# Turning four of sixteen scan inputs with TensorE, and widening GpSimd's share of the products

## The chip, the cores and the metric

The kernel runs on one NeuronCore of a Trainium2 chip. The metric is the device time of one execution in microseconds. Engines are named PE (TensorE), DVE (VectorE), ACT (ScalarE), POOL (GpSimd) and SP (the engine that issues most DMAs).

## The reference

Two layers of a vision network of state-space scans work on x of 8 × 192 × 64 × 64. Each is `x + layer(group_norm(x))`. The first layer (layer 0 in the code, phase s0, 384 channels) projects and convolves the image, reads it in K = 4 directions of L = 4096 steps, and runs this scan for every channel d and each of N = 16 states n:

```python
delta = softplus(dt + bias)
h[n] = exp(delta * A[n]) * h[n] + (delta * u) * B[n]
y = sum over n of h[n] * C[n]
```

```python
ys = ys + Ds.reshape(K, Din)[None, :, :, None] * u
y = ys[:, 0] + ys[:, 2, :, ::-1]
yt = ys[:, 1] + ys[:, 3, :, ::-1]
```

yt is turned back to row order and added, and norm and projection follow. The second layer (layer 1 in the code, phase s1, 128 channels, 3 branches) runs the same sort of scan once per branch. B, C and the rank-12 part of dt come from a projection of u. Everything is fp32.

## The kernel before

The program is a chain of phases: features of the first layer, its scans, its output, then the same three for the second. `scan_phase` serves both layers. In the first, nd = 3 tiles of 128 channels lie side by side (J = 3), a step takes T = 512 time steps, and a **unit** g is one direction of one image in one chunk of 512 steps: 8 × 4 × 8 = 256 units, one after another. Units 0 to 7 of an image are direction 0, and so on; those of directions 2 and 3 "fold": they add the reversed result of directions 0 and 1, which is loaded again into `prev`. In the second layer J = 2 (two states at once), and there are 192 units of 8 states.

A unit of the first layer, for each of 16 states s:

- ACT computes the decays exp(delta × A) for 3 tiles, into a ring of DECAYS = 3 PSUM slots `dA` (L769). Decay (s, j) waits until the scan three tiles earlier is over.
- POOL forms `dbu` = du × B for 3 tiles at once (L845, 128 × 1536), AHEAD = 4 states in front of the scans. B comes as rows broadcast to 128 partitions by DMA into `b_sb`. Behind state s − 4's scans it multiplies that state's last tile by C (L855).
- DVE runs three scans (`tensor_tensor_scan`, L908, first operand decay, second dbu, start value `state`), and, behind the first scan of the next state, multiplies tiles 0 and 1 by C (L918; C in PSUM as `c_ps`). State 8 is an exception: POOL has no share, and DVE multiplies 3 tiles.
- PE spreads the C row over the partitions (L631), and sums h·C over the states into `y_ps` with identity matmuls: `state_sum` for DVE's products (L641), `pool_sum` for POOL's, three states later (L649).
- ACT saves the last column of h as the next unit's start value after every 2 states (L776).

Work for the next unit is placed by hand at states, in the dicts `on_pe`, `on_act`, `on_pool`: xproj (L587) at state 0 of PE and its copy at state 2 of ACT, dt (L605) at 3 to 5, softplus (L753, between two table loads L750 and L758) at 7, the three scalings of the identity by D (`scale_ident`, L721) at 8, corrections of the bf16 rows (`rest`, L595 and L596) at 8 and 10. POOL forms du = delta × u (L863) at 11. `direct` (L614) opens each unit's sum with D·u, for tiles 0 and 1 at state 1, for tile 2 at state 3, after ACT has copied the unit before out of PSUM (L732 at state 1, L738 at state 4), and L621 adds prev in folding units. ACT issues the store of `yo` at state 6.

All engines work in order. SP's queue does too: per unit it issues C part 1, prev (if the next unit folds), B part 2, the store of the next unit's rows, B part 3, C parts 2 and 3, B parts 0 and 1 and C part 0 of the next unit, then the loads of unit g + 2. A part is 4 rows × 512, broadcast to 1 MB. `h` holds 4 states, so a scan also waits for the products of four states before.

PE's order within a state:

```python
for s in range(NS):
    ...
    c_broadcast(g, s)
    if s == 1:
        direct(g, range(OWN), evacuated)
    if s:
        state_sum(g, s - 1)
    ...
    if nd > 1 and s == LAG:
        direct(g, (nd - 1,), evacuated_pool)
    if s >= LAG and s - LAG in SHARE:
        pool_sum(g, s - LAG)
```

## Time and profile before

| | |
|---|---|
| Time, median of 3 runs | 28,545.9 us (28,539.72 to 28,559.49) |
| Profiled execution, span | 28,546.6 us |
| DVE busy | 26,177.2 us (92%) |
| POOL busy | 24,984.9 us (88%) |
| PE busy | 23,745.5 us (83%), granted clock 0.970 |
| ACT busy | 15,919.5 us (56%) |
| All 15,296 recorded scans (L908) | 18,924.0 us |
| POOL's 5634 input products and du (L845) | 17,651.6 us |
| DMA | 4580.79 MB, mean 160 GB/s |

The span runs from the first to the last instruction, and stands within 1 us of the median time. A record's duration can overlap the next one's on the same engine by some hundredths to tenths of a microsecond, so two records' starts give the pace better than their durations. The scans of the first layer run from about 1070 to 20560 us of the span.

### The profile page before, as it was taken

What the parts mean: (1) busy time and instruction counts of PE and PEld (TensorE: products, weight loads), DVE (VectorE), ACT (ScalarE), POOL (GpSimd) and SP (SyncE); (2) the same over time, 40 slices, a digit from 0 to 9 for tenths busy, and PEclk for the clock granted to TensorE, in tenths of its full rate; (3) what the DMA queues carried; (4) which work ended last, traced back from release to release, by engine and by line L of the source; (5) the groups of instructions that cost most, each with busy time, mean ns of one, the idle gap of its engine ahead of it and who ended that gap; (6) DMA issues with size and microseconds to landing.
All of it is one profiled execution on the core that took longest, in us unless ns stands there. A gap on an engine that the chain in (4) does not pass through costs nothing. (4 is left out here: it accounts for less than half of the span.)

```text
span 28546.6 us, 217771 instructions
## 1 busy us (share of the span) xinstructions
PE 23745.5 (83%) x55698; PEld 9094.3 (32%) x55698; DVE 26177.2 (92%) x22479; ACT 15919.5 (56%) x25927; POOL 24984.9 (88%) x10936
## 2 busy tenths in 40 slices
PE   8778878887887887788788788878789988888888
PEld 3333333333333333333333333333334433333332
DVE  8899999999999999999999999999952179999996
ACT  2455555555555555555555555555522356666663
POOL 1699999999999999999999999999802179999995
PEclk9899999999999999999999999999999999999999
DMA  6533333333333333333333333333452357777778
GB/s 202 188 133 147 143 135 138 146 138 136 143 143 136 141 145 136 139 145 137 137 145 143 133 140 146 138 133 148 158 176 84 102 193 229 231 230 230 229 230 292
DMA packets 1193779, 4580.79 MB, mean 160 GB/s; under 512 B 254080, under 2 KB 291984, under 8 KB 827184
## 3 DMA queue, kind: packets, MB, share of 16 engines
q1 hardware_dynamic: 1093280, 4217.64, 41.8%
q10 hardware_dynamic: 99248, 349.22, 3.3%
q8 instruction: 450, 7.37, 0.1%
q14 instruction: 801, 6.56, 0.1%
HBM read 3907.76 MB, written 658.64 MB: 160 GB/s over the span
## 5 line engine op out<-in xcount | busy, mean ns | idle before, releaser
L908 DVE TENSOR_TENSOR_SCAN s_h<-s_dA,s_state,s_dbu 128x512 f32<-128x512 f32 x15296 | 18924.0, 1314 | 257.2 <-ACT s_dA L769 254.2
L845 POOL TENSOR_TENSOR s_dbu<-s_du,s_b_sb 128x1536 f32<-128x1536 f32 (+1 forms) x5634 | 17651.6, 3139 | 4.8 <-DVE s_h L908 3.1
L769 ACT ACTIVATE s_dA<-s_delta,s_negA 128x512 f32<-128x512 f32 x15360 | 10502.0, 690 | 8824.5 <-DVE s_h L908 8791.8
L641 PE MATMUL s_y_ps<-s_hc,s_ident 128*128 128x512 f32 x21504 | 10652.8, 617 | 1.5 <-DVE s_hc L918 1.5
L918 DVE TENSOR_TENSOR s_hc<-s_h,s_c_ps 128x1024 f32<-128x1024 f32 (+2 forms) x5632 | 6809.5, 1209 | 17.8 <-PE s_c_ps L631 12.3
L855 POOL TENSOR_TENSOR s_hc_pool<-s_h,s_c_sb 128x512 f32<-128x512 f32 x4608 | 5835.6, 1266 | 206.2 <-DVE s_h L908 202.3
L631 PE MATMUL s_c_ps<-s_bc,s_sel 96*128 96x512 bf16 x6400 | 2373.9, 390 | 3886.2 <-DVE s_hc L918 3883.7
L641 PEld LDWEIGHTS s_y_ps<-s_hc,s_ident 128*128 128x128 f32 x21504 | 4255.1, 198 | 3245.8 <-issue 3030.4
L649 PE MATMUL s_y_ps<-s_hc_pool,s_ident 128*128 128x512 f32 x9216 | 4789.6, 602 | 0.0
L631 PEld LDWEIGHTS s_c_ps<-s_bc,s_sel 96*128 96x128 bf16 x6400 | 569.2, 96 | 7635.9 <-DVE s_hc L918 6533.2
L649 PEld LDWEIGHTS s_y_ps<-s_hc_pool,s_ident 128*128 128x128 f32 x9216 | 1811.4, 197 | 2347.3 <-issue 2319.8
L1528 POOL TENSOR_TENSOR f_row_sum<-f_pad 96x1056 f32<-96x1056 f32 x64 | 155.1, 2424 | 1997.4 <-DVE f_pad L1475 1400.3
L863 POOL TENSOR_TENSOR s_du<-s_delta,s_u 128x1536 f32<-128x1536 f32 (+1 forms) x450 | 1126.5, 2503 | 190.1 <-ACT s_delta L756 146.0
L614 PE MATMUL s_y_ps<-s_u,s_D_ident 128*128 128x512 f32 x1920 | 973.8, 610 | 354.9 <-ACT s_yo L738 293.7
L605 PE MATMUL s_prep_ps<-s_xd,s_wdt 12*128 12x512 f32 (+1 forms) x1928 | 1083.7, 642 | 4.6 <-ACT s_bc L708 2.5
L1491 DVE TENSOR_TENSOR f_cen<-f_ps,f_middle 64x512 f32<-64x512 f32 x64 | 43.7, 682 | 1128.5 <-issue 672.2
L587 PE MATMUL s_prep_ps<-s_u,s_wx 128*108 128x512 f32 (+1 forms) x1928 | 910.6, 598 | 108.8 <-DMA s_keep_in<-in_keep 92.3
L776 ACT ACTIVATE s_state<-s_h,s_keep 128x6 f32<-128x6 f32 (+1 forms) x2432 | 724.2, 298 | 448.4 <-DVE s_h L908 439.7
L595 PE MATMUL s_prep_ps<-s_xd,s_twice 32*64 32x512 f32 x1800 | 963.9, 615 | 5.9 <-ACT s_delta L753 3.7
L311 DVE SCALAR_TENSOR_TENSOR f_row<-f_pad,f_taps,f_row 128x4096 f32<-128x4096 f32 x128 | 651.3, 5088 | 4.6
L750 ACT ACT_TABLE_LOAD x450 | 577.4, 1283 | 8.1
L758 ACT ACT_TABLE_LOAD x450 | 577.4, 1283 | 8.1
(162 smaller groups left out, 13497.4 us busy)
## 6 DMA issues: line engine op xcount, KB each, us to landing
s_b_sb<-rows SPq DMA_DIRECT2D x1794, 1024.0 KB, 5.0
s_c_sb<-rows SPq DMA_DIRECT2D x1216, 1024.0 KB, 6.6
s_u<-U SPq DMA_DIRECT2D x257, 768.0 KB
Y<-s_yo ACTq DMA_DIRECT2D x256, 768.0 KB, 5.5
s_prev<-Y SPq DMA_DIRECT2D x128, 768.0 KB, 6.1
s_u<-U SPq DMA_DIRECT2D x193, 256.0 KB
U<-f_row SPq DMA_DIRECT2D x24, 2048.0 KB, 17.3
U<-f_col SPq DMA_DIRECT2D x24, 2048.0 KB, 7.1
```

Source lines behind the costliest of these rows:

```text
L595: pe.matmul(prep_ps[0:64, :], twice[:, :], xd[0:32, :], start=True, stop=False)
L605: pe.matmul(prep_ps[:, :], wdt[g % 2][XROWS:XROWS + rank, t, :], xd[XROWS:XROWS + rank, :], start=True, stop=True).then_inc(dt_done, 1)
L614: last = pe.matmul(y_ps[:, t, :], D_ident[q][:, t, :], u[q][:, t, :], start=True, stop=False)
L631: last = pe.matmul(c_ps[:, r, :], sel[:, s * ng + r, :], bc16[g % 2][:, :], start=True, stop=True)
L641: last = pe.matmul(y_ps[:, t, :], ident[:, :], hc[:, s % 2, j, :], start=False, stop=nd > 1 and s == NS - 1)
L649: pe.matmul(y_ps[:, nd - 1, :], ident[:, :], hc_pool[:, (m - 1) % 4, :], start=False, stop=s == SHARE[-1]).then_inc(summed_pool, 1)
L769: act.activation(dA[:, n % DECAYS, :], delta[g % 2][:, t, :], ACT.Exp, scale=negA[g % 2][:, a:a + 1]).then_inc(dA_ready, 1)
L845: pool.tensor_tensor(dbu[:, s % AHEAD, :, :], a, b, ALU.mult).then_inc(dbu_ready, 1)
L855: pool.tensor_tensor(hc_pool[:, m % 4, :], h[:, s % (2 * GROUP), J - 1, :], c_sb[:, part % 2, row % ROWS_IN, :], ALU.mult).then_inc(hcp_re ...
L863: pool.tensor_tensor(du[q][:, :, :], delta[q][:, :, :], u[q][:, :, :], ALU.mult).then_inc(du_ready, 1)
L908: dve.tensor_tensor_scan(h[:, s % (2 * GROUP), j, :], dA[:, (n * J + j) % DECAYS, :], dbu[:, s % AHEAD, j, :], initial, ALU.mult, ALU.add) ...
L918: dve.tensor_tensor(hc[:, s % 2, 0:own, :], h[:, s % (2 * GROUP), 0:own, :], c, ALU.mult).then_inc(hc_ready, 1)
```

## The change

In the first layer's scans:

- States 3, 7, 11 and 14 (TURNED) no longer have their input formed by POOL. Once a unit, PE transposes the B and C rows (`turn_rows`) and the three tiles of du (`turn_du`), so that time lies on the partitions, and ACT copies them to SBUF (`take_rows`, `take_du`). For each turned state ACT multiplies the four blocks of 128 time steps of du by that state's B, which is then one value per partition (`scale_du`, 128 × 384, four per state), and PE transposes the result, tile by tile, back into a slot of the PSUM ring `dA` (`turn_input`, four transpositions per tile). The decays of these states go to SBUF (`dA_sb`), and the scan reads decay from SBUF and input from PSUM. `SCALE_AT` says at which states ACT does the scalings, `on_pe` and `on_act` where the turning of rows and du stands (states 11 to 15).
- POOL multiplies the last two tiles by C, in place of one, for states 2, 3, 6, 7, 10, 11 (TWO); state 8 now has a share like the others. DVE's products shrink by as many tiles.
- D is summed over the four directions and applied once, in direction 0's units; other units open their sum with prev or with the first product. The identity is scaled by D once per phase.
- `yo` and `prev` have one buffer in place of two, `hc` holds two tiles.

In the second layer TURNED and TWO are empty, and what remains is the single scaling of the identity and the one `yo`.

The diff, cut to what the prediction speaks of:

```diff
     C_STATES = tuple(range(NS)) if nd > 1 else (0, 2, 4, 6)
-    SHARE = tuple(s for s in C_STATES if nd == 1 or s != 8)
+    SHARE = C_STATES
     NSH = len(SHARE)
+    TWO = (2, 3, 6, 7, 10, 11) if nd > 1 else ()
+    POOL_TILES = 2 if nd > 1 else 1
     LAG = 3 if nd > 1 else 2
+    TURNED = (3, 7, 11, 14) if nd > 1 else ()
+    NT = len(TURNED)
+    PLAIN = tuple(s for s in range(NS) if s not in TURNED)
+    NPL = len(PLAIN)
+    QB = T // 128
+    SCALE_AT = {3: (0, 0, 1, 1), 7: (3, 4, 5, 5), 11: (7, 8, 9, 9), 14: (10, 11, 12, 12)}
...
-    on_pe = (dict(xproj=0, dt=(3, 4, 5), mid=8, low=10) if nd > 1 else
+    on_pe = (dict(xproj=0, dt=(3, 4, 5), mid=8, low=10, rows=11, turn_du=(12, 13, 14)) if nd > 1 else
              dict(xproj=0, dt=(2,), mid=4, low=5))
-    on_act = (dict(evacuate=1, take=2, evacuate_pool=4, dt=(4, 5, 6), store=6, soft=7, scale_ident=8, mid=9, low=11)
+    on_act = (dict(evacuate=1, take=2, evacuate_pool=4, dt=(4, 5, 6), store=6, soft=7, mid=9, low=11, rows=12, turn_du=(13, 14, 15))
               if nd > 1 else
-              dict(evacuate=2, take=2, soft=4, store=4, scale_ident=5, mid=6, low=7))
+              dict(evacuate=2, take=2, soft=4, store=4, mid=6, low=7))
     on_pool = dict(du=11 if nd > 1 else 7)
...
+    def opens(g):
+        return nd == 1 or g // NCH % K == 0
+    def opened_before(g):
+        return sum(1 for x in range(g) if opens(x))
+    def pool_tiles(s):
+        return 2 if s in TWO else 1 if s in SHARE else 0
     def in_product(s):
-        return J - 1 if s in SHARE else J
+        return J - pool_tiles(s)
...
+    def inputs_before(n):
+        return n // NS * NPL + sum(1 for x in PLAIN if x < n % NS)
+    def state_of_input(i):
+        return i // NPL * NS + PLAIN[i % NPL]
...
-        yo = [sb(f"yo{q}", [128, nd, T]) for q in range(2)]
-        D_ident = [sb(f"D_ident{q}", [128, nd, 128]) for q in range(2)]
-        prev = [sb(f"prev{q}", [128, nd, T]) for q in range(2 if BACK else 0)]
+        yo = sb("yo", [128, nd, T])
+        D_in, D_ident = sb("D_in", [128, K, nd]), sb("D_ident", [128, nd, 128])
+        if BACK:
+            prev = sb("prev", [128, nd, T])
+        if NT:
+            duT, rowsT = sb("duT", [128, QB, nd * 128]), [sb(f"rowsT{q}", [128, QB, 32]) for q in range(2)]
+            scaled_du, dA_sb = sb("scaled_du", [128, 2, QB, nd * 128]), sb("dA_sb", [128, J, T])
...
                 f, other = fold_of(g), partner(g)
-                wait(eng, prev_summed, f - 1)
-                eng.wait_ge(stored[other % 2], 16 * (other // 2 + 1))
-                eng.dma_start(prev[f % 2][:, :, :], Y[other]).then_inc(prev_in[f % 2], 16)
+                wait(eng, prev_summed, f)
+                eng.wait_ge(stored, 16 * (other + 1))
+                eng.dma_start(prev[:, :, :], Y[other]).then_inc(prev_in, 16)
...
-                wait(eng, dbu_ready, g * NS + (part + 1 - B_RING) * STEPS_IN)
+                wait(eng, dbu_ready, inputs_before(g * NS + (part + 1 - B_RING) * STEPS_IN))
...
+            def turn_rows(g):
+                pe.wait_ge(xd_ready, g + 1)
+                pe.wait_ge(bc_ready, g * 3 + 3)
+                for b in range(QB):
+                    last = pe.transpose(prep_ps[:, b * 32:(b + 1) * 32], xd[0:32, b * 128:(b + 1) * 128], ident[0:32, 0:32])
+                last.then_inc(rows_turned, 1)
+            def turn_du(g, t):
+                pe.wait_ge(du_ready, g + 1)
+                if t == 0:
+                    pe.wait_ge(rows_taken, g + 1)
+                else:
+                    pe.wait_ge(du_taken, g * nd + t)
+                for b in range(QB):
+                    last = pe.transpose(prep_ps[:, b * 128:(b + 1) * 128], du[g % 2][:, t, b * 128:(b + 1) * 128], ident[:, :])
+                last.then_inc(du_turned, 1)
+            def turn_input(g, s, j):
+                m, n = turn_of(g, s), (g * NS + s) * J + j
+                pe.wait_ge(du_scaled, (m + 1) * QB)
+                wait(pe, scanned, n - DECAYS + 1)
+                for b in range(QB):
+                    last = pe.transpose(dA[:, n % DECAYS, b * 128:(b + 1) * 128],
+                                        scaled_du[:, m % 2, b, j * 128:(j + 1) * 128], ident[:, :])
+                last.then_inc(input_turned, 1)
             def direct(g, tiles, read):
-                q = g % 2
-                pe.wait_ge(D_ready, g + 1)
                 wait(pe, read, g)
-                for t in tiles:
-                    last = pe.matmul(y_ps[:, t, :], D_ident[q][:, t, :], u[q][:, t, :], start=True, stop=False)
-                if tiles[-1] == nd - 1:
-                    last.then_inc(direct_done, 1)
+                if opens(g):
+                    for t in tiles:
+                        last = pe.matmul(y_ps[:, t, :], D_ident[:, t, :], u[g % 2][:, t, :], start=True, stop=False)
+                    if tiles[-1] == nd - 1:
+                        last.then_inc(direct_done, 1)
                 if folds(g):
-                    f = fold_of(g)
-                    pe.wait_ge(prev_in[f % 2], 16 * (f // 2 + 1))
+                    pe.wait_ge(prev_in, 16 * (fold_of(g) + 1))
                     for t in tiles:
-                        last = pe.matmul(y_ps[:, t, :], ident[:, :], prev[f % 2][:, t, ::-1], start=False, stop=False)
+                        last = pe.matmul(y_ps[:, t, :], ident[:, :], prev[:, t, ::-1], start=True, stop=False)
...
-                pe.matmul(y_ps[:, nd - 1, :], ident[:, :], hc_pool[:, (m - 1) % 4, :],
-                          start=False, stop=s == SHARE[-1]).then_inc(summed_pool, 1)
+                tiles = pool_tiles(s)
+                for i in range(tiles):
+                    last = pe.matmul(y_ps[:, nd - tiles + i, :], ident[:, :], hc_pool[:, (m - 1) % 4, i, :],
+                                     start=begins(g, s), stop=s == SHARE[-1])
+                last.then_inc(summed_pool, 1)
...
+                    if NT and s == on_pe["rows"]:
+                        turn_rows(g + 1)
+                    if NT and s in on_pe["turn_du"]:
+                        turn_du(g + 1, on_pe["turn_du"].index(s))
+                    if s + 1 in TURNED:
+                        turn_input(g, s + 1, 0)
                     c_broadcast(g, s)
                     if s == 1:
                         direct(g, range(OWN), evacuated)
                     if s:
                        state_sum(g, s - 1)
                     elif g:
                         state_sum(g - 1, NS - 1)
+                    if s + 1 in TURNED:
+                        turn_input(g, s + 1, 1)
                     if nd > 1 and s == LAG:
                         direct(g, (nd - 1,), evacuated_pool)
                     if s >= LAG and s - LAG in SHARE:
                         pool_sum(g, s - LAG)
                     elif s < LAG and g and NS + s - LAG in SHARE:
                         pool_sum(g - 1, NS + s - LAG)
+                    if s + 1 in TURNED:
+                        turn_input(g, s + 1, 2)
...
+            def take_rows(g):
+                act.wait_ge(rows_turned, g + 1)
+                act.activation(rowsT[g % 2][:, :, :], prep_ps[:, 0:QB * 32].rearrange("p (b n) -> p b n", n=32),
+                               ACT.Copy).then_inc(rows_taken, 1)
+            def take_du(g, t):
+                act.wait_ge(du_turned, g * nd + t + 1)
+                wait(act, du_scaled, g * NT * QB)
+                act.activation(duT[:, :, t * 128:(t + 1) * 128], prep_ps[:, :].rearrange("p (b d) -> p b d", d=128),
+                               ACT.Copy).then_inc(du_taken, 1)
+            def scale_du(g, s, b):
+                m = turn_of(g, s)
+                act.wait_ge(rows_taken, g + 1)
+                act.wait_ge(du_taken, (g + 1) * nd)
+                wait(act, input_turned, (m - 1) * J)
+                act.activation(scaled_du[:, m % 2, b, :], duT[:, b, :], ACT.Copy,
+                               scale=rowsT[g % 2][:, b, s:s + 1]).then_inc(du_scaled, 1)
...
-                wait(act, stored[q], 16 * (g // 2))
-                place = yo[q][:, 0:OWN, ::-1] if folds(g) else yo[q][:, 0:OWN, :]
+                wait(act, stored, 16 * g)
+                place = yo[:, 0:OWN, ::-1] if folds(g) else yo[:, 0:OWN, :]
...
-                wait(act, scanned, n - DECAYS + 1)
+                if s in TURNED:
+                    m = turn_of(g, s)
+                    if m:
+                        act.wait_ge(scanned, turned_state(m - 1) * J + j + 1)
+                    place = dA_sb[:, j, :]
+                else:
+                    wait(act, scanned, n - DECAYS + 1)
+                    place = dA[:, n % DECAYS, :]
                 a = t * N_STATE + s * ng + r
-                act.activation(dA[:, n % DECAYS, :], delta[g % 2][:, t, :], ACT.Exp,
+                act.activation(place, delta[g % 2][:, t, :], ACT.Exp,
...
-                wait(pool, scanned, (n - AHEAD + 1) * J)
+                i = inputs_before(n)
+                if i >= AHEAD:
+                    pool.wait_ge(scanned, (state_of_input(i - AHEAD) + 1) * J)
                 a, b = du[g % 2][:, :, :], b_sb[:, s % (B_RING * STEPS_IN), :, :]
                 a, b = (a, b.broadcast_to([128, nd, T])) if ng == 1 else (a.broadcast_to([128, ng, T]), b)
-                pool.tensor_tensor(dbu[:, s % AHEAD, :, :], a, b, ALU.mult).then_inc(dbu_ready, 1)
+                pool.tensor_tensor(dbu[:, i % AHEAD, :, :], a, b, ALU.mult).then_inc(dbu_ready, 1)
...
-                pool.tensor_tensor(hc_pool[:, m % 4, :], h[:, s % (2 * GROUP), J - 1, :],
-                                   c_sb[:, part % 2, row % ROWS_IN, :], ALU.mult).then_inc(hcp_ready, 1)
+                tiles = pool_tiles(s)
+                c = c_sb[:, part % 2, row % ROWS_IN:row % ROWS_IN + 1, :].broadcast_to([128, tiles, T])
+                pool.tensor_tensor(hc_pool[:, m % 4, 0:tiles, :], h[:, s % (2 * GROUP), J - tiles:J, :], c,
+                                   ALU.mult).then_inc(hcp_ready, 1)
...
-                    input_of(g + s // NS, s % NS)
+                    if s % NS in PLAIN:
+                        input_of(g + s // NS, s % NS)
...
+                if s in TURNED:
+                    dve.wait_ge(input_turned, turn_of(g, s) * J + j + 1)
+                    decay, given = dA_sb[:, j, :], dA[:, (n * J + j) % DECAYS, :]
+                else:
+                    i = inputs_before(n)
+                    decay, given = dA[:, (n * J + j) % DECAYS, :], dbu[:, i % AHEAD, j, :]
+                    if j == 0:
+                        dve.wait_ge(dbu_ready, i + 1)
...
-                dve.tensor_tensor_scan(h[:, s % (2 * GROUP), j, :], dA[:, (n * J + j) % DECAYS, :],
-                                       dbu[:, s % AHEAD, j, :], initial, ALU.mult, ALU.add).then_inc(scanned, 1)
+                dve.tensor_tensor_scan(h[:, s % (2 * GROUP), j, :], decay, given, initial,
+                                       ALU.mult, ALU.add).then_inc(scanned, 1)
```

## Rows read from the trace of the kernel before

**Rows 1.** Stretch table, 6000 to 12000 us: busy us (x count) by engine, then clock.

```profile
6000.00:12000.00 6000.00, 4836.43 (x10912) 1849.91 (x10911) 5921.34 (x5045) 3540.24 (x5829) 6000.00 (x2523) 0.97 0.37 139
```

**Rows 2.** Groups of instructions by shape, 6000 to 18000 us: busy us, mean ns, idle.

```profile
L908 DVE TENSOR_TENSOR_SCAN s_h<-s_dA,s_state,s_dbu 128x512 f32<-128x512 f32 x7566 | 9183.4, 1273 | 158.3 <-ACT s_dA L769 155.3 <-POOL s_dbu L845 3.0
...
L845 POOL TENSOR_TENSOR s_dbu<-s_du,s_b_sb 128x1536 f32<-128x1536 f32 x2523 | 8665.9, 3435 | 0.0
...
L641 PEld LDWEIGHTS s_y_ps<-s_hc,s_ident 128*128 128x128 f32 x10401 | 2077.2, 200 | 1646.9 <-issue 1580.3
...
L721 ACT ACTIVATE s_D_ident<-s_ident,s_small 128x128 f32<-128x128 f32 x471 | 153.2, 388 | 0.0
...
L738 ACT ACTIVATE s_yo<-s_y_ps 128x512 f32<-128x512 f32 x157 | 90.9, 579 | 0.0
```

**Rows 3.** Timeline of DVE around state 8 of a unit: start us, us.

```profile
10027.97 2.46 DVE L908 TENSOR_TENSOR_SCAN s_h<-s_dA,s_state,s_dbu 128x512 f32<-128x512 f32 x2
10031.44 1.28 DVE L908 TENSOR_TENSOR_SCAN s_h<-s_dA,s_state,s_dbu 128x512 f32<-128x512 f32 x1 [1.01 <-ACT s_dA L769]
10032.64 1.20 DVE L918 TENSOR_TENSOR s_hc<-s_h,s_c_ps 128x1024 f32<-128x1024 f32 x1
10033.75 3.63 DVE L908 TENSOR_TENSOR_SCAN s_h<-s_dA,s_state,s_dbu 128x512 f32<-128x512 f32 x3
10037.30 1.73 DVE L918 TENSOR_TENSOR s_hc<-s_h,s_c_ps 128x1536 f32<-128x1536 f32 x1
10038.94 3.63 DVE L908 TENSOR_TENSOR_SCAN s_h<-s_dA,s_state,s_dbu 128x512 f32<-128x512 f32 x3
```

**Rows 4.** Timeline of POOL, one state of the first layer.

```profile
9003.82 1.26 POOL L855 TENSOR_TENSOR s_hc_pool<-s_h,s_c_sb 128x512 f32<-128x512 f32 x1
9005.05 3.42 POOL L845 TENSOR_TENSOR s_dbu<-s_du,s_b_sb 128x1536 f32<-128x1536 f32 x1
9008.44 1.26 POOL L855 TENSOR_TENSOR s_hc_pool<-s_h,s_c_sb 128x512 f32<-128x512 f32 x1
```

**Rows 5.** Groups by shape in the second layer, 22000 to 28546 us.

```profile
L845 POOL TENSOR_TENSOR s_dbu<-s_du,s_b_sb 128x1024 f32<-128x1024 f32 x1537 | 3583.2, 2351 | 4.6 <-DVE s_h L908 3.1 <-DMA s_b_sb<-rows 1.5
...
L918 DVE TENSOR_TENSOR s_hc<-s_h,s_c_ps 128x1024 f32<-128x1024 f32 x768 | 1079.6, 1406 | 2.1 <-PE s_c_ps L631 1.4 <-DVE s_h L908 0.7
...
L918 DVE TENSOR_TENSOR s_hc<-s_h,s_c_ps 128x512 f32<-128x512 f32 x768 | 669.4, 872 | 10.7 <-PE s_c_ps L631 10.7
```

**Rows 6.** Timeline of ACT from decay (6,2) to decay (8,0), the same unit as rows 3.

```profile
10021.16 0.69 ACT L769 ACTIVATE s_dA<-s_delta,s_negA 128x512 f32<-128x512 f32 x1 [0.48 <-DVE s_h L908]
...
10021.79 0.67 ACT L744 ACTIVATE s_work<-s_prep_ps,s_small 128x512 f32<-128x512 f32 x1
10022.36 0.29 ACT L776 ACTIVATE s_state<-s_h,s_keep 128x6 f32<-128x6 f32 x1
...
10026.53 1.28 ACT L750 ACT_TABLE_LOAD   x1
...
10029.32 1.28 ACT L758 ACT_TABLE_LOAD   x1
10030.62 1.92 ACT L769 ACTIVATE s_dA<-s_delta,s_negA 128x512 f32<-128x512 f32 x3
```

**Rows 7.** Timeline of PE, one state: an x4 row is four matmul records.

```profile
9001.42 1.88 PE L641 MATMUL s_y_ps<-s_hc,s_ident 128*128 128x512 f32 x4
9003.14 1.02 PE L649 MATMUL s_y_ps<-s_hc_pool,s_ident 128*128 128x512 f32 x2
...
9006.58 0.38 PE L631 MATMUL s_c_ps<-s_bc,s_sel 96*128 96x512 bf16 x1
9006.80 1.88 PE L641 MATMUL s_y_ps<-s_hc,s_ident 128*128 128x512 f32 x4
```

**Rows 8.** DMA issues, 6000 to 18000 us: count, size, median us to landing.

```profile
s_b_sb<-rows SPq DMA_DIRECT2D x631, 1024.0 KB, 4.7
...
s_prev<-Y SPq DMA_DIRECT2D x80, 768.0 KB, 6.1
```

More of the change, by code:

```diff
@@ L462, in scan_phase @@
         loaded = [sem(f"loaded{q}") for q in range(2)]
-        stored = [sem(f"stored{q}") for q in range(2)]
+        stored = sem("stored")
         xproj_done, rest_done, bc_ready, minus_set = sem("xproj_done"), sem("rest_done"), sem("bc_ready"), sem("minus_set")
@@ L574, in _ @@
                         broadcast_b(g + 1, 3)
-            for q in range(2):
-                eng.wait_ge(stored[q], 16 * (units // 2))
+            eng.wait_ge(stored, 16 * units)
             eng.wait_ge(rows_stored, 16 * (units + 1))
@@ L623, in direct, with begins @@
                         last.then_inc(prev_summed, 1)
+            def begins(g, s):
+                return s == 0 and not opens(g) and not folds(g)
             def c_broadcast(g, s):
@@ L641, in state_sum @@
                     last = pe.matmul(y_ps[:, t, :], ident[:, :], hc[:, s % 2, j, :],
[L642 removed]
+                                     start=begins(g, s), stop=nd > 1 and s == NS - 1)
                 last.then_inc(summed, 1)
@@ L683, in _ @@
                 rest(0, part)
+            if NT:
+                turn_rows(0)
+                for t in range(nd):
+                    turn_du(0, t)
             for g in range(units):
@@ L811, in unit @@
                         take_rest(g + 1, 1)
+                    if NT and s == on_act["rows"]:
+                        take_rows(g + 1)
+                    for x in TURNED:
+                        for b in range(QB):
+                            if SCALE_AT[x][b] == s:
+                                scale_du(g, x, b)
+                    if NT and s in on_act["turn_du"]:
+                        take_du(g + 1, on_act["turn_du"].index(s))
                     if s == on_act["store"] and g:
@@ L820, in _ @@
             softplus(0)
-            scale_ident(0)
             for part in range(2):
                 take_rest(0, part)
+            if NT:
+                take_rows(0)
+                for t in range(nd):
+                    take_du(0, t)
             for g in range(units):
@@ L884, in _ @@
         def _(dve):
-            dve.wait_ge(const_in, 32)
+            dve.wait_ge(const_in, 48)
+            for k in range(1, K):
+                dve.tensor_tensor(D_in[:, 0, :], D_in[:, 0, :], D_in[:, k, :], ALU.add).then_inc(D_summed, 1)
+                dve.wait_ge(D_summed, k)
+            dve.sem_inc(D_summed, 1)
             dve.tensor_copy(sel[:, :, :].rearrange("p a b -> p (a b)"), self32).then_inc(sel_ready, 1)
```

74 lines of the change are left out of this document (41 added, 33 removed).

## The prediction

> **What bounds the kernel now.** I read the stretch table first, then the groups of instructions, then the timelines of single engines. From 6000 to 12000 us VectorE (DVE) is busy for 5921 us and GpSimd (POOL) for all 6000, while ScalarE (ACT) has 3540 and TensorE (PE) 4836, at a granted clock of 0.97 of 2.4 GHz [rows 1]. 7566 scans stand in 12,000 us; a unit has 48, so a unit takes 12,000 × 48 / 7566 = 76.13 us, and layer 0's 256 units take 19.5 of the 28.5 ms [rows 2].
>
> VectorE: three scans start within 3.55 us (1.183 each), a product of two tiles takes 1.11 and one of three tiles 1.64 [rows 3]. 48 × 1.183 + 15 × 1.11 + 1.64 = 75.1 us, and before the scan of state 8 it waits 1.01 us for a decay [rows 3]: 76.1. GpSimd: product 1.23 us, input product 3.39 us from start to start [rows 4]; du is taken as an input product. 16 × 3.39 + 15 × 1.23 + 3.39 = 76.1. Both are full, but the scans waited 155 us for ScalarE and only 3 us for GpSimd [rows 2]: VectorE's own sequence, with its wait, sets the period, and GpSimd keeps pace with nothing to spare. A change has to relieve both.
>
> **The change, part by part.** I write S_n for the start of state n's first scan on VectorE. A state takes 3.55 + 1.11 = 4.66 us; where the product inside it (that of the state before) has one tile it is shorter.
>
> VectorE. Six states give a second tile's product to GpSimd, and state 8 gives its first. Removing a tile saves 1.64 − 1.11 = 0.53 us [rows 3]; the narrow product itself is not in layer 0, but in layer 1 it differs from the wide one by 1406 − 872 = 534 ns [rows 5]. 7 × 0.53 = 3.7 us. The narrow product is then 0.58, and the state around it takes 4.13. Scans of the four turned states read the decay from SBUF and the input from PSUM, the reverse of now. No row shows that; the bounds are zero and one narrow product's reading (0.53 us, 12 times, 6 us); I take zero, since such a scan still reads one tile from each memory, as today's does. VectorE without waits: 75.1 − 3.7 = 71.4.
>
> GpSimd. Four inputs go, −4 × 3.39 = −13.6. State 8's product comes, +1.23; six products become two tiles wide, each by half of 3.39 − 1.23 = 2.16, so +1.08 and +6.5 (layer 1's input product of two tiles, 2351 ns, agrees with 1.23 + 1.08 [rows 5]). 76.1 − 13.6 + 7.7 = 70.2: below VectorE.
>
> ScalarE. A scaling of 128 columns takes 388 ns as a record [rows 2], the decay of 512 columns 690 [rows 6]; for 384 columns that gives 0.59, some 0.5 from start to start. 16 of these (9.4), three copies of du (0.58 each, as L738's copy of 512 columns out of PSUM [rows 2]), one of the rows (0.25), less three scalings of the identity (1.2): +10.2 on 3540 / 6000 × 76.13 = 44.9 [rows 1], so 55 of 71: hidden by sum. By order: today the softplus with its two table loads (4.09 us) sits behind decay (7,2), which can only start when its PSUM slot is free; that is the wait of 1.01 us. State 7 is now turned and its decays go to SBUF, so they needn't wait for a scan. The first row of rows 3 holds scans (7,1) and (7,2), so S_6 was 10027.97 − 2.29 − 4.66 = 10021.02, and decay (6,2) starts at S_6 + 0.14 [rows 6]; then follow dt copy and state save (0.8 in all), three decays (1.85), tables and softplus (4.09), the first scaling for state 11 (0.5), and decay (8,0), ready at about S_6 + 8.85. State 8 is due at S_6 + 4.66 + 4.13 = S_6 + 8.79. So 0.1 us of the 1.01 stays. What is late next is the scaling work; I went through ACT's order state by state, and every other scaling stands at least 2 us ahead of the transposition that takes it.
>
> TensorE. Two matmul records make one fp32 product of 512 columns; four start within 1.72 us, so 0.43 each, and a bf16 one takes 0.22 [rows 7]. A unit now has 48 products of h·C (41.3 us), 3 of u with x_proj, 3 of dt, 3 direct, on average 1.5 of the earlier result (9.0), 16 C rows in bf16 (3.5) and two corrections (2.2): 56.0. Three of four direct groups go: 54.1. Added: 60 transpositions of 128 × 128 and 4 short ones, at x each. The trace of before has none. Lower bound: a quarter of 0.22, 0.055. Upper: two passes, each a weight load of 0.20 [rows 2] and 128 columns (0.107) in turn, 0.61. I take one pass of 128 columns at fp32's pace, 0.107, nearest to the row of the same type: weight loads lie beside running matmuls in rows 7 (four start within 1.72 us though each has its load), and I take it that the second pass of an fp32 product serves the multiplication, which a transposition has not. Sum 54.1 + 64 × 0.107 = 61 of 71.
>
> The Trainium skill (TensorE: Matmul & The Clock Gate, Part 4: PE-mode transpose) speaks against this: some 390 ns for a bf16 transpose alone and 275 in a kernel, and the full clock isn't engaged by transposes. By 0.275, an estimate, TensorE's sum would be 71.7, above VectorE's. Its section Terms calls transpose mode four times faster for fp32, which would give 0.053 by rows 7. No row here decides between them.
>
> TensorE's order matters more than its sum, as three transposed tiles per turned state are interleaved with other products, and VectorE waits for each. Tightest is state 11. From the end of product 8 at S_9 + 2.3: C row 0.22, state_sum(8) 1.72, pool_sum(6) 1.72 (two tiles now), rest 1.08, four transpositions, C row 0.22, state_sum(9) 1.72, four transpositions, pool_sum(7) 1.72, four transpositions: 8.4 + 12x. Tile 2's scan is due at S_11 + 2.95 = S_9 + 12.3, so 10.0 are there: x up to 0.13 costs nothing. At 0.107 the margin is 0.3 us; I allow 0.1 for hand-overs. The same count gives 5.1 + 16x against 8.1 for state 14 (up to 0.19, with du's transposition ahead), 8x against 1.6 for state 7 (0.20) and 7.3 + 12x against 10.0 for state 3 (0.22).
>
> SP queue. With one prev buffer, load_prev(g+1) waits until prev of unit g is summed, about S_4 + 2.3 (ScalarE's evacuation after decay (4,2), then two passes). Queued behind it are B's part 2, the row store, B's part 3 and C's part 2. A B part lands 4.7 us after issue and prev 6.1 [rows 8]; in a row I put B's part at S_4 + 10. GpSimd would like it at S_5 + 1.3, so it comes to stand 4 to 5 us late; by its own times (70.2 a unit) input 12 is where that lateness is nearest to the scans, and it reaches them if the part lands after about S_4 + 11. I count 0. It can concern 120 of 256 units (those that fold and are followed by one that folds). The single yo buffer: the store of unit g−1 is issued at state 6 and lands before the next evacuation, most of a unit later: nothing. Layer 1 loses one scaling of 0.39 us per unit on ScalarE, which waits for scans there: nothing. The start gains some 5 us of turning, once.
>
> **Sum.** 71.4 + 0.1 + 0.1 = 71.6 us a unit, 4.53 less; × 256 = 1160; + 5. The profiled execution's 28,546.6 becomes 27,392; I say 27,400. Its span is within 1 us of the median of 28,545.9.
>
> **Rivals.**
> - *The wait on ScalarE stays* because the added scalings cost more than 0.5 or start late: +0.9 us a unit, 27,630. For: the chain at state 8 has no reserve. Against: the decays of state 7 are freed by a whole state. Chance 0.14.
> - *Transpositions take two passes*, x = 0.21: state 11 is 1.0 late, 14 0.4, 7 0.1: +1.4 after the 0.1 allowed, 27,760. For: every fp32 product in rows 7 does so. Chance 0.14.
> - *The held SP queue starves GpSimd*: a landing 3 us after the limit costs 120 × 3 = 360 us, 27,760. For: three 1 MB transfers and prev come in one burst. Chance 0.08.
> - *Other side: TensorE's turning sets the period.* If weight load and columns follow one another, x = 0.20 + 0.107 = 0.30; the late tiles cost 2.0 (state 11), 1.8 (14), 0.8 (7), 0.7 (3, in three of four units): 5.3, so 76.8 us a unit and 28,720. It decides from x = 0.28, where the waits eat all 4.5 us; in two passes of 0.21 TensorE's sum alone would be 81, 29,900. For: each transposition has another weight, of 0.20 us. Against: loads lie beside matmuls today. Chance 0.06. The skill's 0.275 as a price is this rival's edge, the waits 4.2 us, 28,490; for it I keep 0.03.
> - *The inputs aren't relieved* (scans slower from swapped memories): 0.02.
>
> The forecast has 0.53. The range: below, 27,300, if the scans or products come out 0.3 us a unit cheaper; above, 27,800, which takes in the first three rivals and leaves out some 0.13. Under 0.2% (57 us) a measurement can't tell from no change. Faster 0.92, same 0.02, slower 0.06.
>
> **What would show it.** In the new profile: scans of layer 0 at 1.18 apart also for the four turned states; narrow products of 0.58 apart; GpSimd with idle time in front of products, released by scans; transpose records and their spacing (0.107 or 0.21); VectorE's waits by releaser: on dA by ScalarE near 0.1 us a unit, on the transposed tiles near 0.1 at state 11, on dbu none. Waits of 1 us and more on transposed tiles show TensorE's rivals; waits on dbu in units 17 to 31 of each image, with b_sb landing late, the SP queue. I am wrong if the unit is longer than 72.5 us.

## The result and the profile after

The changed kernel takes 27,906.65 us (median of 4 runs, 27,883.81 to 27,921.66) against 28,545.42: a ratio of 0.9775, with a 95% interval of 0.9763 to 0.9787. It is faster by 639 us, where 1146 were forecast, and lies above the range. Times here are medians of a kernel's undisturbed executions; one of the four of e2_prev_late took 61,744 us at a granted clock of 0.41 and is left out.

Engines' totals on the page of the profiled execution (span 27,919.9 us):

```profile
PE 24874.1 (89%) x70946; PEld 10612.0 (38%) x70946; DVE 25291.2 (91%) x22482; ACT 17866.2 (64%) x30091; POOL 23560.1 (84%) x10168
```

The stretch table, as in [rows 1]: VectorE busy 5835 of 6000, GpSimd no longer full, TensorE from 4836 to 5367.

```profile
6000.00:12000.00 6000.00, 5367.45 (x16151) 2401.87 (x16150) 5835.04 (x5211) 4297.78 (x7405) 5744.51 (x2364) 0.98 0.38 144
```

Groups by shape, 6000 to 18000 us, as in [rows 2]. 5863 scans of plain states, 36 a unit, make a unit of 12,000 × 36 / 5863 = 73.7 us, against 76.13 before and 71.6 forecast.

```profile
L1049 DVE TENSOR_TENSOR_SCAN s_h<-s_dA,s_state,s_dbu 128x512 f32<-128x512 f32 x5863 | 7151.4, 1265 | 38.2 <-ACT s_dA L884 32.3 <-POOL s_dbu L971 2.4
...
L1049 DVE TENSOR_TENSOR_SCAN s_h<-s_dA_sb,s_state,s_dA 128x512 f32<-128x512 f32 x1955 | 2438.0, 1266 | 191.0 <-PE s_dA L672 188.9 <-ACT s_dA L884 1.8
...
L830 ACT ACTIVATE s_scaled_du<-s_duT,s_rowsT 128x384 f32<-128x384 f32 x2606 | 1496.6, 605 | 6.1
...
L672 PE MATMUL s_dA<-s_ident,s_scaled_du 128*128 128x128 f32 x7819 | 1183.2, 274 | 26.6 <-DVE s_h L1049 26.6
...
L672 PEld LDWEIGHTS s_dA<-s_ident,s_scaled_du 128*128 128x128 f32 x7817 | 954.7, 141 | 934.5 <-issue 905.6 <-ACT s_scaled_du L830 26.9
```

The scans of turned states take as long as the others (1266 and 1265 ns), a scaling 605 ns. Each transposition is one matmul record of 274 ns and one weight load of 141. VectorE's timeline in a unit of direction 1, as in [rows 3], at state 11:

```profile
9169.53 1.25 DVE L1049 TENSOR_TENSOR_SCAN s_h<-s_dA_sb,s_state,s_dA 128x512 f32<-128x512 f32 x1
9170.70 0.66 DVE L1059 TENSOR_TENSOR s_hc<-s_h,s_c_ps 128x512 f32<-128x512 f32 x1
9171.28 1.27 DVE L1049 TENSOR_TENSOR_SCAN s_h<-s_dA_sb,s_state,s_dA 128x512 f32<-128x512 f32 x1
9172.95 1.28 DVE L1049 TENSOR_TENSOR_SCAN s_h<-s_dA_sb,s_state,s_dA 128x512 f32<-128x512 f32 x1 [0.40 <-PE s_dA L672]
```

The narrow product runs from 9170.70 to the next scan's start at 9171.28, 0.58 us, and the third turned scan waits 0.40 us for its transposed input. That is the one recorded wait in this unit, which takes 71.9 us. Its price is a little more than the wait: 1.67 us lie between the starts of the second and the third scan (9171.28 to 9172.95) where 1.18 is the pace, so 0.49. Waits in total, 6000 to 18000 us (us, times, longest):

```profile
POOL s_dbu L971 <- DMA s_b_sb<-rows: 264.5, 75, 4.7
...
DVE s_h L1049 <- PE s_dA L672: 188.9, 357, 3.0
...
PE s_prep_ps L626 <- DMA s_keep_in<-in_keep: 108.9, 67, 3.2
...
DVE s_hc L1059 <- issue: 90.7, 64, 3.9
...
DVE s_h L1049 <- ACT s_dA L884: 34.0, 45, 0.9
```

VectorE waits 188.9 us for transposed inputs and 90.7 in front of products, where nothing else is named than the missing C row. With the smaller ones it is 329 us in 163 units, 2.0 us a unit.

**Units by direction.** ACT starts the softplus once a unit; the distance from one start to the next, averaged by the direction to which the unit belongs, is this (us; 64 units each, 63 for direction 0):

| kernel | dir. 0 | dir. 1 | dir. 2 | dir. 3 | time, us |
|---|---|---|---|---|---|
| before | 76.19 | 76.13 | 76.14 | 76.13 | 28,545 |
| changed | 73.48 | 72.86 | 74.22 | 74.10 | 27,907 |
| e3_turn_first | 71.64 | 72.23 | 73.93 | 74.17 | 27,753 |
| e4_fill | 71.89 | 71.90 | 73.93 | 74.20 | 27,738 |
| e1_evac3 | 72.23 | 72.19 | 72.45 | 72.56 | 27,592 |
| e2_prev_late | 73.72 | 72.93 | 73.48 | 73.71 | 27,889 |
| e8_fill_prev | 71.89 | 71.90 | 71.90 | 71.90 | 27,480 |
| e7_all | 71.65 | 71.64 | 71.79 | 71.64 | 27,424 |
| e9_all_fill | 71.38 | 71.39 | 71.39 | 71.39 | 27,348 |
| e5_no_two | 74.43 | 74.47 | 74.46 | 74.46 | 28,127 |
| e10_before_fill | 76.18 | 76.13 | 76.41 | 76.41 | 28,582 |

Directions 2 and 3 fold and load prev, direction 0 applies D, direction 1 does neither. In the changed kernel some units of directions 0 and 1 take 71.9 us, others 75.0. Here is PE in one of the latter, of direction 0:

```profile
10611.71 1.74 PE L681 MATMUL s_y_ps<-s_u,s_D_ident 128*128 128x512 f32 x2 [1.35 <-ACT s_yo L846]
10613.24 1.92 PE L721 MATMUL s_y_ps<-s_hc_pool,s_ident 128*128 128x512 f32 x2
10615.09 1.31 PE L644 MATMUL s_prep_ps<-s_xd,s_wdt 12*128 12x512 f32 x2
10616.33 0.39 PE L701 MATMUL s_c_ps<-s_bc,s_sel 96*128 96x512 bf16 x1
...
10636.00 0.61 PE L701 MATMUL s_c_ps<-s_bc,s_sel 96*128 96x512 bf16 x1 [2.48 <-DVE s_hc L1059]
10636.40 3.37 PE L711 MATMUL s_y_ps<-s_hc,s_ident 128*128 128x512 f32 x4
```

An idle stretch of 1.35 us, waiting for the evacuation of tile 2, ends at 10611.71. The two records that follow start 1.53 us apart from the next row in place of 0.86, and two more take until 10615.09. At 10636.40 four records have 3.37 us where four had 1.88. The stretch table of the same unit says why; the number after the five engines is the granted clock:

```profile
9130.00:9202.00 72.00, 62.84 (x195) 28.07 (x194) 71.57 (x65) 52.99 (x92) 70.69 (x30) 1.00 0.37 141
...
10611.70:10615.30 3.60, 3.59 (x5) 1.19 (x6) 3.60 (x4) 3.11 (x6) 2.74 (x2) 0.55 0.62 214
...
10636.00:10639.40 3.40, 3.40 (x5) 1.67 (x6) 3.40 (x3) 2.23 (x4) 3.40 (x3) 0.50 1.01 417
```

0.50 is TensorE at 1.2 GHz in place of 2.4, for some 3.5 us, twice in this unit. Both times it had stood idle just before (1.35 and 2.48 us). In the unit of 9130 us it stands idle 1.64 us at the first of these places and 2.55 us at the second (9162.64, shown further down), and there the clock stays at 1.00 (first row of the table): not every such pause is followed by a fall. PE in that unit, with four transpositions between a `state_sum` and a `pool_sum`, and the pause:

```profile
9134.00 0.60 PE L672 MATMUL s_dA<-s_ident,s_scaled_du 128*128 128x128 f32 x4
9134.44 1.02 PE L721 MATMUL s_y_ps<-s_hc_pool,s_ident 128*128 128x512 f32 x2
...
9139.78 1.12 PE L721 MATMUL s_y_ps<-s_hc_pool,s_ident 128*128 128x512 f32 x2 [1.64 <-ACT s_yo L846]
```

What VectorE waits for in the unit of 10600 us:

```profile
10616.81 1.22 DVE L1059 TENSOR_TENSOR s_hc<-s_h,s_c_ps 128x1024 f32<-128x1024 f32 x1 [1.10 <-issue]
...
10628.25 1.28 DVE L1049 TENSOR_TENSOR_SCAN s_h<-s_dA_sb,s_state,s_dA 128x512 f32<-128x512 f32 x1 [0.25 <-PE s_dA L672]
...
10643.45 1.28 DVE L1049 TENSOR_TENSOR_SCAN s_h<-s_dA_sb,s_state,s_dA 128x512 f32<-128x512 f32 x1 [0.48 <-PE s_dA L672]
...
10645.82 1.28 DVE L1049 TENSOR_TENSOR_SCAN s_h<-s_dA_sb,s_state,s_dA 128x512 f32<-128x512 f32 x1 [0.52 <-PE s_dA L672]
10647.98 1.28 DVE L1049 TENSOR_TENSOR_SCAN s_h<-s_dA_sb,s_state,s_dA 128x512 f32<-128x512 f32 x1 [0.88 <-PE s_dA L672]
```

The first loss of some 1.7 us of matmul time shows up as 1.10 us before a product and 0.25 at state 7; the second makes all three tiles of state 11 late, 0.48 + 0.52 + 0.88 us. Together 3.2, where the unit at 9130 us loses 0.40.

In stretches of 1 us between 9000 and 11500 us, the kernel before has 46 falls below 0.95 of the clock in 33 units, and its units of directions 1 to 3 all take 76.12 to 76.15 us. The changed one has 27 in 34 units. The falls aren't new; there was nothing that waited for them. Over all units of the first layer but the first and the last the changed kernel has 67 falls in direction 0, 29 in direction 1, 52 in 2 and 69 in 3.

### The profile page after: what moved, and what is told of

The parts are those of the page before. It is cut to its first block and busy times, and to the rows that moved or that the text cites. A ratio compares the mean times of both kernels' runs of the same rounds, so it can differ in the third digit from the quotient of the medians.

```text
span 27919.9 us, 261599 instructions
## 1 busy us (share of the span) xinstructions
PE 24874.1 (89%) x70946; PEld 10612.0 (38%) x70946; DVE 25291.2 (91%) x22482; ACT 17866.2 (64%) x30091; POOL 23560.1 (84%) x10168
## 5 line engine op out<-in xcount | busy, mean ns | idle before, releaser
L1049 DVE TENSOR_TENSOR_SCAN s_h<-s_dA,s_state,s_dbu 128x512 f32<-128x512 f32 x12236 | 14960.7, 1269 | 59.2 <-ACT s_dA L884 50.7
L971 POOL TENSOR_TENSOR s_dbu<-s_du,s_b_sb 128x1536 f32<-128x1536 f32 (+1 forms) x4610 | 14188.6, 3084 | 430.9 <-DMA s_b_sb<-rows 428.7
L884 ACT ACTIVATE s_dA<-s_delta,s_negA 128x512 f32<-128x512 f32 x12288 | 8289.9, 685 | 5515.3 <-DVE s_h L1049 5501.6
L711 PE MATMUL s_y_ps<-s_hc,s_ident 128*128 128x512 f32 x17920 | 8785.2, 602 | 1.5 <-DVE s_hc L1059 1.5
L983 POOL TENSOR_TENSOR s_hc_pool<-s_h,s_c_sb 128x512 f32<-128x512 f32 (+1 forms) x4864 | 7843.8, 1617 | 575.4 <-DVE s_h L1049 514.6
L1059 DVE TENSOR_TENSOR s_hc<-s_h,s_c_ps 128x1024 f32<-128x1024 f32 (+1 forms) x5632 | 5526.0, 981 | 169.5 <-issue 140.9
L1049 DVE TENSOR_TENSOR_SCAN s_h<-s_dA_sb,s_state,s_dA 128x512 f32<-128x512 f32 x3060 | 3816.0, 1266 | 295.1 <-PE s_dA L672 290.8
L830 ACT ACTIVATE s_scaled_du<-s_duT,s_rowsT 128x384 f32<-128x384 f32 x4096 | 2352.4, 605 | 9.6
L884 ACT ACTIVATE s_dA_sb<-s_delta,s_negA 128x512 f32<-128x512 f32 x3072 | 1982.1, 710 | 0.0
L672 PE MATMUL s_dA<-s_ident,s_scaled_du 128*128 128x128 f32 x12288 | 1859.3, 274 | 42.6 <-DVE s_h L1049 42.6
```

Source lines behind the costliest of these rows:

```text
L672: last = pe.transpose(dA[:, n % DECAYS, b * 128:(b + 1) * 128], scaled_du[:, m % 2, b, j * 128:(j + 1) * 128], ident[:, :])
L711: last = pe.matmul(y_ps[:, t, :], ident[:, :], hc[:, s % 2, j, :], start=begins(g, s), stop=nd > 1 and s == NS - 1)
L830: act.activation(scaled_du[:, m % 2, b, :], duT[:, b, :], ACT.Copy, scale=rowsT[g % 2][:, b, s:s + 1]).then_inc(du_scaled, 1)
L884: act.activation(place, delta[g % 2][:, t, :], ACT.Exp, scale=negA[g % 2][:, a:a + 1]).then_inc(dA_ready, 1)
L971: pool.tensor_tensor(dbu[:, i % AHEAD, :, :], a, b, ALU.mult).then_inc(dbu_ready, 1)
L983: pool.tensor_tensor(hc_pool[:, m % 4, 0:tiles, :], h[:, s % (2 * GROUP), J - tiles:J, :], c, ALU.mult).then_inc(hcp_ready, 1)
```

## The experiments

Four explanations of the 2.1 us a unit that separate 73.7 from 71.6 stood against one another: falls of TensorE's clock, which push its transposed tiles and C rows past a thin margin (theory 1); the SP queue held by prev, with loads that come late (2); the order of TensorE's work alone, late at any clock (3); and TensorE's load as such, which more work would make worse (4).

**e3_turn_first.**

```diff
+                    if s + 1 in TURNED:
+                        turn_input(g, s + 1, 2)
                     if s >= LAG and s - LAG in SHARE:
                         pool_sum(g, s - LAG)
...
-                    if s + 1 in TURNED:
-                        turn_input(g, s + 1, 2)
```

> Only PE's order differs from the changed kernel: a turned state's third tile is transposed ahead of the pool_sum of that state, which takes 1.72 us out of the chain that the scan waits for. Theory 1 (half-clock stretches of TensorE make it late, and the chains have too little margin to absorb 1.7 us): the margin grows from 0.3 to about 2 us, so most late third tiles go, in units with a half-clock stretch too: about 27,600 us, with waits of scans for transposed tiles under 0.6 us a unit. Theory 2 (the held SP queue brings loads late): no help in the units that fold, 27,800. Theory 3 (only the thin margin at state 11, 0.4 us in every unit): 27,907 - 256 x 0.4 = 27,805.

27,753 us (ratio 0.9721, 0.9706 to 0.9735), a gain of 153, between theories 1 and 3. By direction it is clearer: directions 0 and 1 gain 1.8 and 0.6 us a unit, more than the 0.5 of state 11, direction 2 gains 0.3 and direction 3 nothing. Waits for transposed inputs fall from 188.9 to 56.7 us. Not all of it is margin: direction 0 has 14 falls of the clock here where the changed kernel has 67. Direction 1 has more of them, 62 against 29, and is faster all the same, so the wider margin does absorb falls. The folding units have another trouble.

**e4_fill**, with `zeros` a bf16 tile of zeros, 0.22 us a matmul.

```diff
+            def keep_busy(count):
+                for _ in range(count if nd > 1 else 0):
+                    pe.matmul(y_ps[:, 0, :], zeros[:, 0:128], zeros[:, :], start=False, stop=False)
...
+                    if s == 9:
+                        keep_busy(9)
                     c_broadcast(g, s)
...
+                    if s == LAG:
+                        keep_busy(6)
```

> Adds 15 bf16 matmuls of zeros by zeros per unit of the first layer (0.22 us each, 3.3 us a unit) where PE stands idle: 6 ahead of the direct group at state 3, 9 ahead of the C row of state 9. They add zero to the sums. Theory 1 (clock): the half-clock stretches behind these two idle places become rare, and although TensorE has 3.3 us more work a unit the time falls, to about 27,650. Theory 4 (TensorE is simply short of time at full clock): more work makes it slower, 28,000 or more. Theory 2 (SP queue): unchanged within 60 us of 27,907.

27,738 us (0.9714, 0.9700 to 0.9729). TensorE does 3.3 us more a unit and the kernel is 169 us faster. All units of directions 0 and 1 but the first take 71.89 to 71.92 us, so theory 4, TensorE's load as such, falls, and the clock holds for them (no fall in either direction, 34 and 41 in directions 2 and 3): the waits left there are the 0.40 of state 11. Directions 2 and 3 stay at 74. What waits there is now mostly the product:

```profile
DVE s_hc L1070 <- issue: 103.2, 48, 4.7
DVE s_h L1060 <- PE s_dA L673: 66.0, 165, 0.4
```

**e1_evac3.**

```diff
-    on_act = (dict(evacuate=1, take=2, evacuate_pool=4, ...
+    on_act = (dict(evacuate=1, take=2, evacuate_pool=3, ...
```

> Only ACT's order differs: the evacuation of tile 2 stands at state 3 in place of 4, so PE no longer waits 1.0 to 1.6 us for it in state 3, and prev is summed some 3 us earlier. Theory 1 (clock): the idle place ahead of the direct group goes, with it the half-clock stretches that begin there, and PE reaches state 5 earlier; the product of state 4 no longer waits for its C row: 27,650 to 27,700. Theory 2: gains only in units that fold, where load_prev is released earlier, 27,750. Theory 3: 27,907, as state 11 is untouched.

27,592 us (0.9663, 0.9646 to 0.9679), a gain of 315, more than theory 1 gave. All directions gain, the folding ones too, as PE isn't stopped at state 3 and prev is free earlier (GpSimd's waits on b_sb fall from 264.5 to 136.9 us). It changes both causes at once and doesn't tell them apart; as a repair it is the best single line.

**e2_prev_late.**

```diff
-                    if folds(g + 1):
-                        load_prev(g + 1)
                     broadcast_b(g, 2)
                     store_rows(g + 1)
                     broadcast_b(g, 3)
+                    if folds(g + 1):
+                        load_prev(g + 1)
```

> Only SP's order differs: load_prev(g+1) is issued behind B part 3 in place of ahead of B part 2, so its wait for the single prev buffer holds nothing up. Theory 2 (the held queue is the cause): waits of POOL for b_sb and of xproj for the loads vanish and the time falls to 27,450. Theory 1 (clock): those waits vanish, but the late tiles stay, above all in direction 0, which loads no prev: 27,850, a gain of at most 0.5 us in half of the units.

27,889 us (0.9766, 0.9750 to 0.9782), not to be told from the changed kernel by the intervals. The folding units gain 0.7 and 0.4 us, the others lose 0.2 and 0.1. TensorE's waits for the loads are all but gone (the row of its weight loads, the only one left, has 7.2 us):

```profile
DVE s_h L1049 <- PE s_dA L672: 214.5, 412, 3.0
...
DVE s_hc L1059 <- issue: 78.0, 71, 1.1
...
PEld s_prep_ps L626 <- DMA s_keep_in<-in_keep: 7.2, 20, 1.0
```

Taken alone this says that the SP queue costs next to nothing. It does cost something, as seen next.

**e8_fill_prev**, the two together.

> The matmuls of zeros of e4_fill together with the SP order of e2_prev_late. With the first alone directions 0 and 1 came to 71.9 us a unit in every unit and directions 2 and 3 stayed at 74; with the second alone nothing moved by more than 0.7. Theory 5 (two causes, each of which hides the other in directions 2 and 3: half-clock stretches, and loads that come late behind the held SP queue): together all four directions come to 71.9, 27,907 - 256 x (73.55 - 71.9) = 27,480. If a third cause keeps directions 2 and 3 slow, they stay above 73 and the time above 27,650.

27,480 us (0.9626, 0.9609 to 0.9642), as expected, and all four directions at 71.9. The granted clock is 1.00, and the waits:

```profile
6000.00:18000.00 12000.00, 11242.17 (x35286) 5090.87 (x35618) 11928.56 (x10682) 8814.26 (x15190) 11783.90 (x4841) 1.00 0.39 148
```

```profile
DVE s_h L1060 <- PE s_dA L673: 66.8, 167, 0.4
...
PE s_prep_ps L627 <- DMA s_keep_in<-in_keep: 1.4, 2, 0.7
```

66.8 us in 167 units is the 0.40 of state 11, and no other wait of VectorE is recorded. Against e4_fill the same edit of the queue that gained 18 us alone, within the noise, now gains 258; against e2_prev_late the filling gains 409, where alone it gained 169. Each cause hid the other in the folding units.

How the queue does harm, in a folding unit of the changed kernel. The first row holds two B parts; SP stays at the second until 9621.93. Behind it come a C part and the loads (u, and as the last keep):

```profile
9601.32 20.61 SPq L566 DMA_DIRECT2D s_b_sb<-rows  x2
...
9622.50 0.38 SPq L537 DMA_DIRECT2D s_u<-U  x1
...
9624.47 0.44 SPq L541 DMA_DIRECT2D s_keep_in<-in_keep  x1
```

PE's xproj needs them and waits 2.82 us. It then takes 4.36 us for six records, 0.73 each where 0.43 is the pace, so this pause too is followed by a lower clock; only behind it comes the C row of state 0:

```profile
9632.38 4.52 PE L626 MATMUL s_prep_ps<-s_u,s_wx 128*108 128x512 f32 x6 [2.82 <-DMA s_keep_in<-in_keep]
9636.74 0.38 PE L701 MATMUL s_c_ps<-s_bc,s_sel 96*128 96x512 bf16 x1
```

VectorE at the same place:

```profile
9628.82 1.26 DVE L1049 TENSOR_TENSOR_SCAN s_h<-s_dA,s_state,s_dbu 128x512 f32<-128x512 f32 x1
...
9637.22 1.22 DVE L1059 TENSOR_TENSOR s_hc<-s_h,s_c_ps 128x1024 f32<-128x1024 f32 x1 [2.48 <-issue]
```

State 0 begins at 9628.82 and the product of state 0 has waited 2.48 us for its C row. The loads were issued 6.3 us before the state began; in the unit of direction 1 at 9130 us they are issued at 9181.75, 10.5 us before the next unit's state 0. The B part ahead of them waits for the unit's last input product, and that GpSimd forms late because an earlier B part reached it late, behind the held load of prev (264.5 us of waits on b_sb in the changed kernel). Putting prev behind the B parts removes this chain.

**e7_all**: evac3, prev late and turn first, no added work.

> No added work: the evacuation of tile 2 at state 3, load_prev behind B part 3, and the third tile's transposition ahead of pool_sum, all three. Theory 5 says that the margin now absorbs a half-clock stretch and that the loads are in time: 71.4 to 71.6 us a unit in all directions, 27,380 (the forecast's 27,400). If half-clock stretches still cost, 27,500.

27,424 us (0.9607, 0.9593 to 0.9621). The least unit is 71.38, the means by direction are 71.64 to 71.79: between the two cases.

**e9_all_fill**, e7_all with nine matmuls of zeros at state 9.

> e7_all with 9 matmuls of zeros ahead of the C row of state 9 (2.0 us a unit). e7_all's units took 71.64 on the mean and 71.38 at the least; what is left above 71.38 are units with a half-clock stretch. Theory 1: all units come to 71.4 and the time to 27,424 - 256 x 0.25 = 27,360. If not, 27,424 as before, or more by the added work.

27,348 us (0.9580, 0.9566 to 0.9594), every unit but the first 71.38 to 71.40 us, and no wait of VectorE is recorded between 6000 and 18000 us (busy 11,995 of 12,000). Direction 1 still has 22 falls of the clock, and its units take no longer: with this order they cost nothing. It beats both kernels, the changed one by 559 us, and is VectorE's own sum with 0.1 us at state 8 (see below).

**e10_before_fill.**

> The kernel before, with the 15 matmuls of zeros of e4_fill per unit of the first layer. Theory 1 says that half-clock stretches cost nothing there, since no scan waits for TensorE and its C rows are early: the granted clock rises from 0.97 towards 1 and the time stays within 30 us of 28,546. If half-clock stretches cost the kernel before as well, the time falls by some of the 1.7 us x 1.4 stretches a unit, by up to 600 us.

28,582 us (1.0014, 1.0004 to 1.0023), 36 us slower, 6 more than expected; and the clock rose only from 0.970 to 0.975, so the run can't tell what a full clock would bring there. Units of directions 2 and 3 grow by 0.27 us; in half of the units ScalarE now waits 0.2 us for dt, which it didn't before, so the added work is the likely reason. That falls of the clock were free in the kernel before rests on its own units of 76.12 to 76.15 us instead.

**e5_no_two and e6_no_turned**, one half of the change each:

```diff
-    TWO = (2, 3, 6, 7, 10, 11) if nd > 1 else ()
+    TWO = ()
```

> The change without its wider share: TWO is empty, the turned states and everything else stay. By the sums, VectorE's unit is 75.1 - 0.5 (state 8's tile) = 74.6 us without waits and GpSimd's 63.7; PE's margin per state grows by half a microsecond where the states are longer. 28,546 - 256 x (76.13 - 74.7) = 28,180. If the turned states' scans were themselves dearer, it would be above 28,300.

28,127 us (0.9853, 0.9834 to 0.9873). All units but two take 74.4 to 74.5 us, in all directions, although GpSimd waits for b_sb here as well (260 us between 6000 and 18000). With the narrow share VectorE's unit is longer, and what is late in the changed kernel comes in time here. The clock has a part in that: it is 1.00 without any filling, with falls in direction 1 alone (20), and the run doesn't tell longer states from the fuller clock.

```profile
6000.00:18000.00 12000.00, 10465.50 (x31988) 4667.40 (x31987) 11999.36 (x10314) 8532.07 (x14662) 10355.88 (x4674) 1.00 0.38 143
```

```diff
-    TURNED = (3, 7, 11, 14) if nd > 1 else ()
+    TURNED = ()
```

> The change without turned states: TURNED is empty, GpSimd forms all 16 inputs and has the wider share as well. By the sums its unit is 76.1 + 7.7 = 83.8 us, above VectorE's 71.4, and it sets the period: 28,546 + 256 x 7.7 = 30,500. If GpSimd were not bound so tightly, below 29,500.

30,504 us, a single execution, against 30,500. GpSimd is busy for all 12,000 us between 6000 and 18000, and VectorE now waits for inputs and for products:

```profile
DVE s_hc L1059 <- issue: 755.0, 197, 5.9
DVE s_h L1049 <- POOL s_dbu L971: 699.9, 591, 3.8
```

The two halves aren't alike. The turned states, with D's and state 8's edits, gain 1.5% without the wider share; the wider share without the turned states costs 7%. Together they gain 2.2% as changed, and 4.2% where nothing is late (e9_all_fill).

## Why the prediction was wrong

- **VectorE's sum, right.** 71.4 us a unit without waits was forecast; 71.38 to 71.39 is the least unit of e3, e7 and e9 (its first unit aside), with some 0.1 of waiting at state 8 in it, so 71.3. The scans with swapped memories cost nothing more (1266 against 1265 ns), the narrow product 0.58.
- **GpSimd's sum, right.** e6_no_turned tests it with the wider share alone: 83.8 a unit forecast, 83.8 in the mean, counted as in the table, and 30,504 us where 30,500 was expected. In the changed kernel it is busy 70.5 us a unit where 70.2 was forecast.
- **ScalarE, right.** A scaling takes 605 ns (0.59 forecast), and ScalarE is busy 53 us in the unit of 9130 us (55 forecast). Of the 1.01 us at state 8, 0.1 was to stay, and 0.1 stays, too little for a wait to be recorded. The first scan of state 8 starts at 9156.07, 2.49 us behind the two before it where such a pair takes 2.37, just after its decay, the first of the three at 9155.26 (0.69 us), is ready; e8_fill_prev and e9_all_fill show the same 0.1:

```profile
9153.58 2.45 DVE L1049 TENSOR_TENSOR_SCAN s_h<-s_dA_sb,s_state,s_dA 128x512 f32<-128x512 f32 x2
9156.07 1.28 DVE L1049 TENSOR_TENSOR_SCAN s_h<-s_dA,s_state,s_dbu 128x512 f32<-128x512 f32 x1
...
9155.26 1.89 ACT L884 ACTIVATE s_dA<-s_delta,s_negA 128x512 f32<-128x512 f32 x3
```

- **The price of a transposition, right.** Four start within 0.44 us (9134.00 to 9134.44 above), so x = 0.11 against 0.107. The rival with two passes falls, and so does serial loading. The Trainium skill's 275 ns, for a bf16 transpose in a kernel (TensorE: Matmul & The Clock Gate, Part 4: PE-mode transpose), isn't the pace here but nearly the length of one fp32 record, 274 ns. That page also says that transposes don't engage the full clock. It can't be seen here: e8_fill_prev has 64 of them a unit at a granted clock of 1.00, but they stand between ordinary matmuls, and no run shows them alone.
- **TensorE's chain at state 11, the step that failed.** "8.4 + 12x against 10.0, the margin is 0.3 us" was worked out at full clock, with 0.1 us allowed for hand-overs. Two things were missing. First, the terms. PE in the unit of 9130 us, clock 1.00:

```profile
9162.64 0.39 PE L701 MATMUL s_c_ps<-s_bc,s_sel 96*128 96x512 bf16 x1 [2.55 <-DVE s_hc L1059]
...
9164.58 1.88 PE L721 MATMUL s_y_ps<-s_hc_pool,s_ident 128*128 128x512 f32 x4
9166.40 1.07 PE L634 MATMUL s_prep_ps<-s_xd,s_twice 32*64 32x512 f32 x2
9167.39 0.40 PE L635 MATMUL s_prep_ps<-s_bc,s_minus 96*64 96x512 bf16 x1
9167.73 0.66 PE L672 MATMUL s_dA<-s_ident,s_scaled_du 128*128 128x128 f32 x4
...
9172.31 0.60 PE L672 MATMUL s_dA<-s_ident,s_scaled_du 128*128 128x128 f32 x4
```

From 9162.64 to the scan at 9172.95 it is 10.31 us where 9.7 were forecast and 9.8 were there, as the C row itself starts 0.14 us behind the point from which the 10.0 were counted. `rest` took 1.33 (1.08 forecast), the last tile 0.64 (0.43), since the scan starts only when the last record is over, and a pool_sum 0.1 more. So where 0.1 was allowed it was 0.49 at full clock, and it stays in every unit of e8_fill_prev. Second, the clock. It was 0.97 [rows 1], which is no even tax of 3%: it is 1.4 stretches a unit in which 1.7 us of matmul time are lost at once. A margin of 0.3 can't hold that. I had priced TensorE by its sum (61 of 71 us; 62.8 of 72 in the unit of 9130 us) and by its order, but not by its order at the clock that the profile gave.
- **The SP queue, right place, wrong reach.** B's part was forecast to leave GpSimd 4 to 5 us late without harm, since the inputs would still be in time. They were (VectorE waited 2.4 us for dbu in 12,000). But the loads of the next unit but one stand behind GpSimd's last input in SP's queue, came 4.2 us later, and PE met them in front of a C row. "I count 0" followed one consumer and stopped: this is the second step that failed. The runs give it 258 us once the clock is out of the way.
- **What the forecast would have been without them.** With both causes gone e8_fill_prev takes 27,480 us, 71.9 a unit, 0.3 above the forecast unit and inside the range.
- **The account.** 27,907 − 27,480 = 427 us for the two causes (e8_fill_prev), 27,480 − 27,348 = 132 for state 11 (e9_all_fill), 0.5 us a unit and so nearly all of it the 0.49. What stays open is how the 427 divide: in folding units either cause alone keeps them slow, so a share for each doesn't exist there.
- **Two prices of rivals.** They don't come out of their own terms: waits of 4.2 us give 27,400 + 256 × 4.1 = 28,450 in place of 28,490, and a sum of 81 us on TensorE gives 28,546.6 + 256 × 4.9 = 29,800 in place of 29,900. Neither rival came about, and nothing else hangs on them.
